# Four stages of a graph network kernel: completion of sums, batch norm and the next table or the sum into x, as one stage per layer on the turned array

## The reference, cut to what matters

```python
# layer 2, after agg = segment_sum(x[src], dst)
h = einsum('nf,hf->nh', x + agg, W) + b
out = (h - mean(h)) * rsqrt(var(h) + 1e-5) * bn_w + bn_b      # mean, var over the nodes
# layer 3 (edges with self loops)
h = relu(gcn_conv(x, W_gcn) + b_gcn)                          # 64 features
h = batch_norm(h, g0, beta0)
h = gat_conv(h, W1, a_src1, a_dst1) + b1                      # 4 heads of 64
h = elu(batch_norm(h, g1, beta1))
h = gat_conv(h, W2, a_src2, a_dst2) + b2
h = elu(batch_norm(h, g2, beta2))
```

## Time and profile before

| | us |
|---|---|
| median of 3 runs | 10042.26 |
| the profiled execution | 10050.07 |
| its span in the trace | 10048.3 |
| PE busy | 5439.5 (54%) |
| PE weight load busy | 4107.3 (41%) |
| POOL busy | 4628.9 (46%) |
| DVE busy | 3953.0 (39%) |
| ACT busy | 3342.3 (33%) |
| DMA, moved | 787.42 MB, 78 GB/s in the mean |

### The profile page before, as it was taken

One profiled execution on the slowest core, in us unless ns is written; L12 is line 12 of the kernel. 1 busy time (PEld: TensorE's weight loads), 2 busy tenths in 40 slices (PEclk: granted clock), 3 DMA queues, 4 the chain that ended last, 5 costly groups with the idle time before them and its releaser, 6 DMA issues. The chain is left out here.

```text
span 10048.3 us, 101926 instructions
## 1 busy us (share of the span) xinstructions
PE 5439.5 (54%) x21038; PEld 4107.3 (41%) x21039; DVE 3953.0 (39%) x8647; ACT 3342.3 (33%) x8076; POOL 4628.9 (46%) x5249
## 2 busy tenths in 40 slices
PE   2279664655533444639643334556564455554397
PEld 1166453444433333526443334244443344443264
DVE  3633475555550000334500000345456454546344
ACT  0042113333332333325333333233332333332253
POOL 4021116555526666233256664566661566651332
PEclk8579866777766777859855555577776777677598
DMA  1224403333323333132211110233331233331323
GB/s 48 99 96 170 148 25 98 90 88 92 89 66 92 93 92 91 32 101 64 91 24 23 23 23 17 83 91 90 88 90 46 79 91 89 91 87 51 101 61 119
DMA packets 431148, 787.42 MB, mean 78 GB/s; under 512 B 132424, under 2 KB 284970, under 8 KB 422834
## 3 DMA queue, kind: packets, MB, share of 16 engines
q0 software_dynamic: 208304, 506.99, 18.4%
q1 hardware_dynamic: 207462, 186.65, 6.3%
q10 hardware_dynamic: 15004, 90.13, 2.2%
HBM read 602.11 MB, written 187.19 MB: 79 GB/s over the span
## 5 line engine op out<-in xcount | busy, mean ns | idle before, releaser
L700 POOL DMA_INDIRECT g_rows<-table,src_idx x2352 | 2231.0, 949 | 1393.5 <-issue 670.6
L971 PE MATMUL g_p_win<-g_rows,g_hot 128*128 128x264 f32 (+1 forms) x4704 | 1544.9, 488 | 43.1 <-issue 35.5
L971 PEld LDWEIGHTS g_p_win<-g_rows,g_hot 128*128 128x128 f32 x4704 | 1100.5, 245 | 305.3 <-issue 68.3
L862 ACT ACTIVATE g_hot<-iota,near 128x128 f32<-128x128 f32 x2352 | 721.0, 387 | 1110.4 <-DMA f_own<-table 515.8
L700 POOL DMA_INDIRECT g2p_rows<-rows,src_idx x784 | 751.4, 958 | 362.2 <-issue 228.3
L700 POOL DMA_INDIRECT gcnp_rows<-table,src_idx x784 | 741.6, 946 | 369.2 <-issue 228.9
L778 DVE TENSOR_TENSOR g_rows<-g_rows,g_p_w 128x1792 f32<-128x1792 f32 x336 | 679.0, 2021 | 36.0 <-issue 5.5
L984 PE MATMUL g_p_f<-ones 1*128 1x4 f32 (+1 forms) x336 | 83.4, 317 | 786.9 <-issue 360.4
L785 DVE TENSOR_TENSOR agg<-agg,g2p_p_out 128x256 f32 x112 | 42.2, 418 | 1099.9 <-PE g2p_p_out L933 637.0
L2035 POOL DMA_INDIRECT back<-e_y,e_idx x210 | 211.0, 1005 | 550.6 <-DVE e_y L2110 546.6
L785 DVE TENSOR_TENSOR agg<-agg,gcnp_p_out 128x64 f32 x112 | 20.3, 221 | 1119.4 <-PE gcnp_p_out L933 852.3
(11 more groups left out here) (667 smaller groups left out, 11844.4 us busy)
## 6 DMA issues: line engine op xcount, KB each, us to landing
g_rows<-table,src_idx POOLq DMA_INDIRECT x2352
expert_rows<-e_zero ACTq DMA_DIRECT2D x28, 1332.5 KB
c_row<-back SPq DMA_DIRECT2D x35, 896.0 KB, 7.5
e_xin<-expert_rows SPq DMA_DIRECT2D x210, 130.0 KB
f_own<-table SPq DMA_DIRECT2D x21, 896.0 KB, 5.0
table<-t_row SPq DMA_DIRECT2D x14, 910.0 KB
expert_rows<-e_zero ACTq DMA_DIRECT2D x10, 1261.0 KB
back<-agg ACTq DMA_DIRECT2D x7, 1792.0 KB, 33.9
```

What stands on the lines that cost most here:

```text
L700: gp.indirect_dma_start(rows[:, s, j, 0:width + H], None, table, bass.IndirectOffsetOnAxis(g.src_idx[:, at:at + 1], 0)).then_inc(got[s], 16)
L862: last = nc.scalar.activation(hot[:, j, :], g.iota[:, :], ACT.Square, scale=-1.0, bias=g.near[:, bass.ds(c * J + j, 1)])
L971: last = nc.tensor.matmul(p_win[:, 0:W], hot[:, j, :], rows[:, s, j, :], start=(j == 0), stop=(j == J - 1))
```

## The change

One function, `turned_norm`, takes the place of `agg_product`, `batch_norm`, three calls of `gat_table` and `gat_finish`, and the layer norm statistics behind A and D. There are four calls of it, one for each of A, B, C and D. It works on groups of four tiles (`QT`; 13 groups, the last of one tile). In a first half the sums are completed with nodes on the partitions, PE turns the tiles, and ACT (DVE for the product of layer 2) evicts them with the bias as a value per partition into `ht`, which has features on the partitions and all nodes along the free dimension. DVE takes statistics of `ht` there. After all groups the mean, variance, scale and shift are worked out, one value per feature and partition. In a second half ACT applies scale and shift (and the exponential); then PE either multiplies `ht` by the table's weights, and rows go to the table and to `inject` as before, or turns the tiles back, and DVE adds them to x and takes the layer norm statistics. The table's weights are prepared inside the first half (`TableWeights`), and the product by the self weight is on POOL. The ring of rows has three slots of four tiles and lies in `g.agg`.

```diff
-    with nc.sbuf_tensor("wt2", [P, 2, D], F32) as g.wt:
-        turned_weights(nc, g, a["L2_gnn_W"], "wt2")
-        agg_product(nc, g, "l2w", g.wt)
-    batch_norm(nc, g, "bnl2", D, a["L2_gnn_b"], a["L2_gnn_bn_w"], a["L2_gnn_bn_b"], True)
-    layernorm_stats(nc, g)
+    turned_norm(nc, g, "nl2", "lin", a["L2_gnn_b"], a["L2_gnn_bn_w"], a["L2_gnn_bn_b"], w=a["L2_gnn_W"])
...
-    batch_norm(nc, g, "bn0", 64, p["b_gcn"], p["g0"], p["beta0"], False, gcn=True)
-    gat_table(nc, g, "t2", p["W1"], p["a_src1"], p["a_dst1"], 4, 64, False, g.table4, g.inject4, False)
+    turned_norm(nc, g, "n0", "gcn", p["b_gcn"], p["g0"], p["beta0"], heads=4, w=p["W1"], table_of=(p["a_src1"], p["a_dst1"]), table=g.table4, inject=g.inject4)
...
-    gat_finish(nc, g, "f2", g.table4, 4, 0.0)
-    batch_norm(nc, g, "bn1", D, p["b1"], p["g1"], p["beta1"], False, elu=True)
-    gat_table(nc, g, "t3", p["W2"], p["a_src2"], p["a_dst2"], 4, D, False, g.table4, g.inject4, False)
+    turned_norm(nc, g, "n1", "gat", p["b1"], p["g1"], p["beta1"], elu=True, heads=4, own_table=g.table4,
+                w=p["W2"], table_of=(p["a_src2"], p["a_dst2"]), table=g.table4, inject=g.inject4)
...
-    gat_finish(nc, g, "f3", g.table4, 4, 0.0)
-    batch_norm(nc, g, "bn2", D, p["b2"], p["g2"], p["beta2"], True, elu=True)
+    turned_norm(nc, g, "n2", "gat", p["b2"], p["g2"], p["beta2"], elu=True, heads=4, own_table=g.table4)
...
+def turned_norm(nc, g, name, kind, bias, gamma, beta, elu=False, heads=0, own_table=None, w=None, table_of=None, table=None, inject=None):
...
+            def _(sp):                                   # sync
...
+                if gat:
+                    for q in range(NB):
+                        own_rows(q)
+                column(0, bias, biased)
+                if not into_x:
+                    tw.load(sp)
+                column(1, gamma, scaled_by)
+                column(2, beta, scaled_by)
+                if gat:
+                    for q in range(NB, NQ):
+                        own_rows(q)                      # waits for mixed, q - NB + 1
+                if not into_x:
+                    for q in range(NQ):
+                        sp.wait_ge(taken, tiles(q)[-1] + 1)
+                        sp.dma_start(table[q * QW:q * QW + width(q), :].rearrange("(t p) d -> p t d", p=P), row[:, q % NB, 0:len(tiles(q)), 0:D + H]).then_inc(stored[q % NB], 16)
...
+            def _(gp):                                   # gpsimd
...
+                    for q in range(NQ):
+                        gp.wait_ge(loaded[q % NB], 16 * (q // NB + 1))
+                        o = heads_of(own[:, q % NB, 0:len(tiles(q)), :])
+                        selfs = g.agg[:, span(q), D + H:D + 2 * H].unsqueeze(3).to_broadcast([P, len(tiles(q)), H, C])
+                        G.tensor_tensor(o, o, selfs, ALU.mult).then_inc(prod, 1)
+                if into_x and elu:
+                    for q in range(NQ):
+                        gp.wait_ge(applied, q + 1)
+                        r = up[:, q % 2, :, 0:real(q)]
+                        G.tensor_scalar(r, r, 0.0, -1.0, ALU.max, ALU.add).then_inc(cut, 1)
+                if not into_x:
+                    for q in range(NQ):
+                        for t in tiles(q):
+                            gp.wait_ge(taken, t + 1)
+                            gp.indirect_dma_start(inject, bass.IndirectOffsetOnAxis(g.first_edge[:, t:t + 1], 0), row[:, q % NB, t - q * QT, D + H:D + 3 * H], None,
+                                                  bounds_check=EP - 1, oob_is_err=False).then_inc(scattered[q % NB], 16)
...
+            def _(pe):                                   # tensor
...
+                else:
+                    for q in range(NQ):
+                        turn(q)                          # waits for fixed q, evicted q - 2
+                        if not into_x and q == 2:
+                            tw.tensor(pe)
+                        if not into_x and q == 4:
+                            tw.tensor_sides(pe)
...
+                    for m in range(NM):                  # pairs of tiles, into x
+                        pe.wait_ge(ready, pair(m)[-1] // QT + 1)
+                        if m >= 2:
+                            pe.wait_ge(added, m - 1)
...
+                            for b in range(FB):          # into the table
+                                last = mm(out[t % 2][:, :], ht[0:kp, b, t * P:(t + 1) * P], tw.rhs[0:kp, b, :], start=(b == 0), stop=(b == FB - 1))
...
+            def _(ac):                                   # scalar
...
+                            last = A.activation(ht[0:kp, b, cols_of(q)], p_t[q % 2][b][0:kp, 0:width(q)], ACT.Relu if gcn else ACT.Identity, bias=vec[0:kp, 0, b:b + 1])
...
+                            A.activation(risen[0:kp, q % 2, b, 0:real(q)], ht[0:kp, b, valid(q)], ACT.Exp, scale=scale[0:kp, b:b + 1], bias=shift[0:kp, b:b + 1])
...
+                        last = A.activation(y, h, ACT.Identity, scale=scale[0:kp, b:b + 1], bias=shift[0:kp, b:b + 1])
...
+            def _(dv):                                   # vector
...
+                        dv.wait_ge(prod, q + 1)
+                        V.tensor_tensor(sums(q), sums(q), own[:, q % NB, 0:len(tiles(q)), :], ALU.add).then_inc(mixed, 1)
+                        dv.wait_ge(mixed, q + 1)
+                        V.tensor_tensor(heads_of(sums(q)), heads_of(sums(q)), inv[:, span(q), :].unsqueeze(3).to_broadcast([P, len(tiles(q)), H, C]), ALU.mult).then_inc(fixed, 1)
...
+                    if not lin and q >= 2:
+                        measure(q - 2)                   # two bn_stats of 512 nodes
...
+                def curve(q):
+                    r = up[:, q % 2, :, 0:real(q)]
+                    if not into_x:
+                        dv.wait_ge(applied, q + 1)
+                        V.tensor_scalar(r, r, 0.0, -1.0, ALU.max, ALU.add).then_inc(cut, 1)
+                    dv.wait_ge(cut, q + 1)
+                    V.scalar_tensor_tensor(out=ht[:, :, valid(q)], in0=risen[:, q % 2, :, 0:real(q)], scalar=1.0, in1=r, op0=ALU.min, op1=ALU.add).then_inc(curved, 1)
...
+                def take(q):
+                    s = q % NB
+                    if q >= NB:
+                        dv.wait_ge(stored[s], 16 * uses(q, s))
+                        dv.wait_ge(scattered[s], 16 * written(q, s))
+                    for t in tiles(q):
+                        dv.wait_ge(product, t + 1)
+                        V.tensor_copy(row[:, s, t - q * QT, :], out[t % 2][:, :]).then_inc(taken, 1)
+                if elu:
+                    curve(0)
+                for q in range(NQ):
+                    if elu and q + 1 < NQ:
+                        curve(q + 1)
+                    if into_x:
+                        for k in range(2 * q, min(NM, 2 * q + 2)):
+                            join(k)
+                    else:
+                        take(q)
```

More of the change, by code:

```diff
@@ L1175, in batch_norm @@
[L1175 to L1192 removed]
+QT = 4
@@ L1244, in _ @@
-                dv.wait_ge(summed, NG)
-                ch.do(V.tensor_scalar(mean[:, :], p_m[:, :], 1.0 / N_NODES, None, ALU.mult))
-                for n in range(NG):
-                    h = g.agg[:, tiles(n), 0:cols]
-                    V.tensor_tensor(h, h, each(mean[:, :]), ALU.subtract).then_inc(less, 1)
-                dv.wait_ge(rooted, 1)
-                ch.do(V.reciprocal(mean[:, :], scale[:, :]))
-                ch.do(V.tensor_tensor(scale[:, :], mean[:, :], wide[:, 1, :], ALU.mult))
@@ new lines, in _ @@
+                if not lin:
+                    measure(NQ - 2)
+                    measure(NQ - 1)
+                ch = Chain(dv, mid)
+                means, spread = (stats[0:kp, :, :, :].rearrange("p b q (e k) -> p b (q e) k", k=3)[:, :, :, k] for k in (1, 2))
+                wide = lambda v: v.unsqueeze(2).to_broadcast([kp, FB, 2 * NQ])
+                shares = share[0:kp, :].unsqueeze(1).to_broadcast([kp, FB, 2 * NQ])
+                m, gp_, pt = mean[0:kp, :], gap[0:kp, :, :], part[0:kp, :, :]
@@ new lines, in _ @@
+                ch.do(V.memset(eps[:, :], BN_EPS), wait=False)
+                ch.do(V.memset(share[:, 0:2 * NQ - 2], QW / 2.0), wait=False)
+                ch.do(V.memset(share[:, 2 * NQ - 2:], tail / 2.0))
+                dv.wait_ge(measured, FB * NQ)
+                ch.do(V.tensor_tensor(pt, means, shares, ALU.mult))
+                ch.do(V.tensor_reduce(out=m, in_=pt, axis=AX.X, op=ALU.add))
+                ch.do(V.tensor_scalar(m, m, 1.0 / N_NODES, None, ALU.mult))
+                ch.do(V.tensor_tensor(gp_, means, wide(m), ALU.subtract))
@@ new lines, in _ @@
+                ch.do(V.tensor_tensor(pt, gp_, shares, ALU.mult))
+                ch.do(V.tensor_tensor(gp_, pt, gp_, ALU.mult))
+                ch.do(V.tensor_tensor(gp_, gp_, spread, ALU.add))
+                ch.do(V.tensor_reduce(out=var[0:kp, :], in_=gp_, axis=AX.X, op=ALU.add))
+                assert ch.n == MEASURED
```

(4 more changed lines are left out.)

348 lines of the change are left out of this document (258 added, 90 removed).

## The result

The changed kernel takes 9725.9 us (median of 4 runs, 9713.9 to 9726.8), the kernel before beside it 10033.2 (4 runs): ratio 0.9687, 95% interval 0.9663 to 0.9711, so 3.1% faster. Forecast were 9700 and a range of 9640 to 9800. The profiled execution has a span of 9723.2 us, 325.1 less than before.

The account below looks back on a forecast made before the run. No engine was busy above 54%; A, C and D were bound by successive VectorE passes with PE's column sums between. Savings of 81, 54, 128 and 81, together 344 us, took 10050.1 to 9706, forecast as 9700; range 9640 to 9800.

Parts of the forecast that it names:

- A: Stage with product, batch norm and layer norm statistics of layer 2; forecast 107.8 us, less by 81.
- D: Stage with f3, batch norm 2 and statistics; forecast 123.4 us, less by 81.
- B: Stage with batch norm 0 and table t2; forecast 102 us, less by 54.
- C: Stage with f2, batch norm 1 and table t3; forecast 149.8 us, less by 128.
- rival 3: Table slots come free too late in B and C: 10 us more in each, 9720 us; chance 0.07.
- rival 1: In C and D, POOL and VectorE operations exclude each other: 36 us more, 9735 us; chance 0.16.
- rival 4: POOL's self product in C and D far dearer than 2.3 us; at 25 us, about 10240; chance 0.02.
- Rival 1's first term: First halves of C and D: POOL's product excludes VectorE's two-input operations, 4.9 us a group, 15 us more in all.
- D, second half: Norm, ELU and addition into x, with POOL's cut max(y, 0) - 1 at 1.1 us: 4.0 us a group, 49 in all.
- rival 1's second term: Second half of D: POOL's cut of 1.1 us can stand before each last ELU step, 13 us more.
- Rival 2: PE's clock stays at 0.50: A's product 45 us more, C's table 25 more, 9770 us; chance 0.11.
- main case: The four stages take their forecast sums, POOL's product mostly overlapping VectorE: gain of 300 to 390 us, chance 0.60.

Follow-up runs that it names:

- the slots run: Changed kernel with 6 slots in the table's ring instead of 3, own rows in 2 buffers in C and 4 in D; ratio 0.9681.
- self_dve: Changed kernel with the product of the self rows in C and D moved back from POOL to VectorE; ratio 0.9646.
- the probe: Changed kernel plus thirteen rounds of POOL and VectorE operations, alone and in pairs, on scratch tiles before B; one execution 9883.0 us.
- pe_join: Changed kernel with PE adding the self rows of C and D in PSUM by identity products, instead of VectorE; ratio 0.9659.
- the control: The changed kernel run again without edits, on another chip; ratio 0.9684.
- no_cut: Changed kernel without D's cut: VectorE forms ELU + 1, and the -1 is added on the way into x; ratio 0.9627.
- cut_dve: Changed kernel with D's cut max(y,0)-1 moved from POOL to VectorE; ratio 0.9636.

## Why the prediction came out as it did

It was right in sign, size and range, and its time is 26 us low. Part of that closeness is luck: C and D alone are 26.6 us over their sums, and A (4.7 under) and the unedited rest (5.8 less) hide a part of that. By its own steps:

- **A.** The product kept its 62 us (61.1 from 4117.4 to 4178.5). The second half was counted at 34.3 and took 30.9: a pair of tiles takes 1.25 us steadily, where I had added up durations with their waits.
- **B.** The first half 23 us (25), the middle 3.7. The scatters took 68.6 us against 62.8, mostly at 1.28 with two double gaps; the slots run shows that it isn't the ring, so rival 3's 10 us in B are not there. On chip 1 the gaps are missing and B, at 99.2 to 99.8, is under its sum.
- **C and D, first half.** 4.3 us a group was forecast, 52.7 in all. Measured are 4.6 in D and 4.9 in C. This is rival 1's mechanism, here shown by self_dve and the probe, and in D by pe_join. POOL's product, taken at 2.3 us, is 1.90 alone, so rival 4 is out and not the price but the overlap was wrong. Rival 1's first term was 15 us over both stages; measured are about 11 (C 70.3 to the middle where 65.1 were forecast, D 66.7 where 60.6 were).
- **C, second half.** 65.8 us for the scatters were forecast, 71.4 measured. I had put 3 us on slots and none on exclusion; the slots run gives the slots 0, the scatters' excess length is 8.8 us, close to rival 1's 8. That closeness is in part chance: rival 1 had the one-input step's length as the cost, and the rows put 2.3 us on that step and 6.3 on scatters that start inside the ELU step. The middle and the start took 12.6 us, not 11.5; the end is 6.3 us, not 7.4.
- **D, second half.** The step that failed most. POOL's cut was taken at 1.1 us within bounds of 1.0 to 2.3, by the row of a memset. Its price alone is 3.7: above the upper bound, since I took the two-input operation as the dearest a POOL instruction of that size could be, and a one-input instruction with two operations is dearer. The half took 72.5 us where 62.8 were forecast, 9.7 of D's 15.8: middle and start 10.5 for 9, the groups (first ELU step to last statistics) 57.8 for 49, the end 4.2 for 4.8. The 49 was itself too high for what VectorE has to do: with no cut the same stretch takes 46.3. So the cut cost the groups 11.5 us and the start 3.7 (10.3 against 6.6), and only the surplus in VectorE's sum kept the miss at 9.7. A part of the 11.5 is rival 1's second term, since ELU steps of 2.05 us and cuts of 4.07 stand in the chain of two groups; how much of it is price and how much exclusion no run separates.
- **The clock.** Rival 2 did not happen in C's second half (0.85 in the control, forecast above 0.8) nor in A's product (0.94 from 4117.4 to 4178.5, before 0.92). A small slip without effect: three loads of 512 KB at the rate of the first are 8.6 us, not 8.4.

So the main case's mechanism won, with rival 1's added to it: 9726 lies nearer to 9735 than to 9700, and I gave it 0.16. The argument that I set against it was no evidence. The gather pass's VectorE operation reads its weight from PSUM (the code makes it a view of a PSUM bank), so it has one input in SBUF, and the addition on POOL ran beside additions from PSUM. By the probe a VectorE operation with one input in PSUM doesn't get in the way of POOL's product. The page of the Trainium skill named there was right that pairs with two SBUF inputs, or the fast one-input step, contend. That the lock is held for the whole instruction fits the two products; it doesn't fit POOL's max and add, during which VectorE ended whole products of 1.22 us.

## What to carry to other kernels

Before work goes from VectorE to POOL, sort both sides by inputs: a VectorE operation with two inputs in SBUF ran in turn with POOL's product and not beside it, and it or the fast one-input form lengthened every kind of POOL instruction that ran beside it here, while statistics and reads from PSUM were free cover. A row only speaks for or against such a rule if it has the same kind of operands, so look up in the code where each input lies. Prices of POOL come from rows of the same form and number of operations, or the bound above has to be left open; and a constant such as ELU's -1 can be free in a later instruction, as in no_cut.

## What the runs showed that I had not expected

- POOL's one-input instruction on 128x1024 is dearer than its product of two tiles: 3.7 us for max and add, 2.8 for max, 2.4 for the product; VectorE does the first in 0.69. The dearer one is also the one that overlaps better with VectorE's products: 4.4 us beside them, with three of them done in that time.
- A POOL scatter that starts inside a two-input VectorE step ends 0.85 us after that step's end, in 28 of 28 cases; started just before, it isn't delayed. The one-input step also catches a scatter that is under way: started 0.43 us before it, the scatter takes 1.23 us. On this the traces go against a remark in the same page of the Trainium skill (SBUF — State Buffer, section Who interferes with whom), which infers that `tensor_tensor` takes only the read interface of the shared pair and so leaves descriptor generation, which needs the write interface, alone. The 28 steps are `scalar_tensor_tensor`; for `tensor_tensor` there is one such case, the first scatter beside VectorE's product, 1.38 us long.
- PE's granted clock in the first halves rose from 0.52 and 0.55 to 0.91 and 0.88 when each transpose became two products with the identity, and D's first half got 10.3 us shorter with the added PE work.
- The same kernel before took 8902 us on one chip and 10050 and 10217 on two others. In the changed kernel on the second, POOL waits 525 us in the gather passes for transfers (147 times, under the name f_own<-table), and the kernel before has 523 us of them in its profiled execution; in cut_dve on the first chip there is no such wait. That is less than half of the difference, and the rest isn't explained.
